# A four-block metaformer on one core: the stages behind the scan are split by image and interleaved

## The reference, cut to what matters

```python
x = x + L0_conv(ln_c(x))            # selective scan over 4 directions, projection
t = t + L0_ffn(ln_t(t))             # mixture of 8 experts, top 2, GELU
x = x + L1_conv(ln_c(x))            # neighbourhood attention, 8 heads, 7x7 window
t = t + L1_ffn(ln_t(t))             # mixture of 8 experts, top 2, GELU
x = x + L2_conv(ln_c(x))            # involution, 3x3, weights made from the pixel
t = t + L2_ffn(ln_t(t))             # switch: 8 experts, top 1, capacity 80, ReLU
x = x + L3_conv(ln_c(x))            # 1x1 projection
t = t + L3_ffn(ln_t(t))             # mixture of 16 gated experts, top 2, SiLU
```

## Time and profile before

| | us |
|---|---|
| median of 3 runs | 360.73 |
| the three runs | 361.05, 355.65, 360.73 |
| the profiled execution, whole | 356.61 |
| its span, first to last instruction | 354.8 |
| TensorE busy | 292.2 (82%) |
| VectorE busy | 233.8 (66%) |
| ScalarE busy | 146.3 (41%) |
| GpSimd busy | 119.7 (34%) |
| granted TensorE clock, mean | 0.901 |

### The profile page before, as it was taken

One profiled execution on the slowest core, in us unless ns is written; L12 is line 12 of the kernel. 1 busy time (PEld: TensorE's weight loads), 2 busy tenths in 40 slices (PEclk: granted clock), 3 DMA queues, 4 the chain that ended last, 5 costly groups with the idle time before them and its releaser, 6 DMA issues.

```text
span 354.8 us, 4098 instructions
## 1 busy us (share of the span) xinstructions
PE 292.2 (82%) x1444; PEld 129.6 (37%) x1452; DVE 233.8 (66%) x468; ACT 146.3 (41%) x285; POOL 119.7 (34%) x72
## 2 busy tenths in 40 slices
PE   6999575665577696785999889998999989987996
PEld 2433111111111232122424589873343733443322
DVE  2308899999999999957415674425155432757784
ACT  1138644433434424240454485524651066303452
POOL 3003467787887876668000043400000100020000
PEclk9699659889759969679699999998999999999998
DMA  7980000000000000013000000000000000000000
GB/s 248 358 310 0 0 3 0 0 1 2 0 0 1 2 0 0 2 32 146 0 2 0 0 3 1 2 0 2 0 1 2 0 2 0 0 0 2 2 0 15
DMA packets 5126, 10.09 MB, mean 28 GB/s; under 512 B 2689, under 2 KB 3265, under 8 KB 4850
## 3 DMA queue, kind: packets, MB, share of 16 engines
q1 hardware_dynamic: 5106, 9.84, 7.8%
HBM read 9.70 MB, written 0.13 MB: 28 GB/s over the span
## 4 chain that ended last, share of the span: by engine, by line
PE 56%; DVE 27%; issue 8%; POOL 3%; ACT 2%; DMA 1%; SPq 1%; DVEq 0%; POOLq 0%; ACTq 0%
DVE arena L1163 14%; PE ps L842 9%; PE ps L822 7%; PE ps L627 5%; DVE arena L1150 4%; PE ps L734 4%; PE ps L953 4%; PE ps L827 2%; PE ps L666 2%; PE ps L941 2%; POOL bias L430 2%; PE ps L861 2%; PE ps L636 2%; PE ps L927 2%; PE ps L808 1%
## 5 line engine op out<-in xcount | busy, mean ns | idle before, releaser
L417 POOL TENSOR_TENSOR arena<-arena 128x1024 f32<-128x1024 f32 x31 | 77.1, 2486 | 29.7 <-DVE arena L1163 25.5
L734 PE MATMUL ps<-arena 32*128 32x510 f32 x128 | 47.7, 827 | 37.1 <-DVE arena L1150 35.4
L1163 DVE TENSOR_TENSOR_SCAN arena<-ps,arena 128x1024 f32<-128x1024 f32 x32 | 73.0, 2281 | 1.6 <-ACT ps L496 1.6
L496 ACT ACTIVATE ps<-ps,aneg 128x510 f32<-128x510 f32 x64 | 39.6, 656 | 69.6 <-PE ps L734 69.6
L740 PE MATMUL ps<-arena 32*128 32x512 f32 x128 | 46.8, 815 | 1.3 <-DVE arena L1150 1.3
L391 POOL TENSOR_TENSOR rstd<-ve,mhalf 128x4 f32<-128x4 f32 (+1 forms) x8 | 8.7, 1089 | 112.2 <-DVE ve L1045 111.5
L1150 DVE TENSOR_TENSOR arena<-ps,arena 128x1024 f32<-128x1024 f32 x32 | 38.8, 1214 | 2.3 <-PE ps L740 1.9
L627 PE MATMUL ps<-idle 128*128 128x512 bf16 x145 | 35.8, 400 | 2.2 <-POOL idle L394 1.3
L734 PEld LDWEIGHTS ps<-arena 32*128 32x128 f32 x128 | 12.2, 229 | 67.6 <-DVE arena L1150 48.6
L458 ACT ACTIVATE xt<-ps 64x256 f32<-64x256 f32 (+1 forms) x8 | 3.0, 381 | 58.9 <-PE ps L636 58.9
L842 PE MATMUL ps<-arena 128*64 128x512 f32 x96 | 25.6, 611 | 0.1
(11 more groups left out here) (215 smaller groups left out, 492.6 us busy)
## 6 DMA issues: line engine op xcount, KB each, us to landing
arena<-in_w SPq DMA_DIRECT2D x5, 512.0 KB, 5.3
bias<-in_rpb SPq DMA_DIRECT2D x1, 1408.0 KB, 8.9
w<-in_w SPq DMA_DIRECT2D x2, 512.0 KB, 7.0
arena<-in_w SPq DMA_DIRECT2D x1, 1024.0 KB, 10.7
c<-in_c SPq DMA_DIRECT2D x1, 740.0 KB, 5.6
arena<-in_w_conv SPq DMA_DIRECT2D x1, 576.0 KB, 4.5
w_bc<-in_w_bc SPq DMA_DIRECT2D x1, 512.0 KB, 5.6
c<-in_c SPq DMA_DIRECT2D x1, 480.0 KB, 6.6
```

Of the source, the lines that this page charges most:

```text
L417: pool.tensor_tensor(hc[:, i % HC_SLOTS], states[i % 4], c_all, ALU.mult).then_inc(hc_done, 1)
L496: act.activation(a, a, ACT.Exp, scale=aneg[:, q:q + 1]).then_inc(exp_done, 1)
L734: pe.matmul(dst, spread[rows_, m], src, start=True, stop=True).then_inc(dspread, 1)
L1163: dve.tensor_tensor_scan(h, decay_banks(i).rearrange("p s l -> p (s l)"), h, 0.0, ALU.mult, ALU.add).then_inc(scan_done, 1)
```

## The change

Everything behind the scan is done per image: an instruction that covered 512 tokens becomes two that cover 256 (`HALF`), and what worked on four tiles works on two (`TPI`). The programs of the engines are interleaved so that one image's norm stands inside the other's expert stage. All `keep_warm` behind the scan goes but one of 17 ahead of the first expert stage (`WARM_NORM = 17`). A few other things change with it:

- A buffer for each hidden block and for each combined quarter (`hid`, `part`): the additions into `acc` on VectorE are gone in the first three expert stages, and TensorE sums four parts per image instead of two sums for both images.
- The weights are spread for two quarters at a time, and ScalarE copies both in one instruction.
- The fourth expert stage handles two experts per step (`gate_mul`, 8 steps per image with 512 columns, `combine_two`).
- GpSimd does the first norm's power ahead of adding the window to the attention bias, which is now cut in 16 pieces.
- The output leaves in two transfers.

The core of it:

```diff
-            def turn(n):
-                if n:
-                    keep_warm(WARM_NORM[n])
-                    turned(n - 1)
-                for t in range(TB):
+            def turn(n, im):
+                for t in of_image(im):
...
-                hidden(0)
...
-                    hidden(1)
-                    down(0)
-                    hidden(2)
-                    down(1)
-                    weights(0)
-                    hidden(3)
-                    weights(1)
-                    down(2)
-                    weights(2)
-                    down(3, between=True)
+                hidden(0)
+                hidden(1)
...
+                down(0)
+                hidden(2)
+                if im == 0:
+                    turn(n, 1)
+                else:
+                    turn(n + 1, 0)
+                down(1)
+                hidden(3)
+                weights(f, im, 0)
+                if stage == 5:
+                    project(0)
+                down(2)
+                weights(f, im, 1)
+                down(3)
+                turned(n + im, 1 - im)
...
+                for p in range(4):
+                    pe.wait_ge(comb, base_c + p + 1)
+                    out_sum(im, part[p], p == 0, p == 3)
...
+            def experts(f, im):
+                n = LN_OF_FFN[f]
+                router_top(f, im)
+                if im == 1:
+                    norm(n + 1, 0)
+                    normed_rows(n + 1, 0)
+                else:
+                    if f:
+                        norm(n, 1)
+                    normed_rows(n, 1)
+                router_rest(f, im)
+                if im == 0:
+                    turned(n)
+                weights_turned(f, im)
+                for p in range(4):
+                    combine(f, im, p)
...
+            for im in range(IMAGES):
+                router_top(3, im)
+                gate_mul(im, 0)
+                if im == 0:
+                    norm(6, 1)
+                else:
+                    finish(3, 0)
+                gate_mul(im, 1)
```

More of the change, by code:

```diff
@@ L655, in _ @@
             last.then_inc(fdt_ps, 1)
-            turn(0)
+            for im in range(IMAGES):
+                turn(0, im)
             got("w_in")
-            turned(0)
+            for im in range(IMAGES):
+                turned(0, im)
             pe.wait_ge(xt_padded, 1)
@@ new lines, in _, with logits_of, weights_turn @@
+            keep_warm(WARM_NORM, 5)
+            turn(1, 0)
+            turned(1, 0)
+            def logits_of(f, im):
+                n = E_OF[f]
+                for t in of_image(im):
+                    last = pe.matmul(bank(7)[:, (t % TPI) * n:(t % TPI + 1) * n], xt[:, t * P:(t + 1) * P], wr[f][:], start=True, stop=True)
+                last.then_inc(logits, 1)
+            def weights_turn(f, im):
+                e_n = E_OF[f]
+                pe.wait_ge(w_ready, IMAGES * f + im + 1)
+                for t in of_image(im):
+                    last = pe.transpose(bank(7).bitcast(BF16)[0:PARTS * e_n, (t % TPI) * P:(t % TPI + 1) * P],
+                                        wp[:, t, 0:PARTS * e_n], ident16)
+                last.then_inc(wt_ps, 1)
@@ new lines, in out_sum @@
+            def out_sum(im, v, first, end):
+                for t in range(TPI):
+                    last = pe.matmul(bank(0)[:, t * CH:(t + 1) * CH], v[:, t * P:(t + 1) * P], stack_i,
+                                     start=(first and t == 0), stop=(end and t == TPI - 1), skip_group_check=True)
+                if end:
+                    last.then_inc(out_ps, 1)
+            def experts(f, im):
+                n = LN_OF_FFN[f]
+                stage = IMAGES * f + im
+                base, base_c = 16 * stage, 4 * stage
+                got(f"wr_{f}", f"w2_{f}", f"w1_{f}")
+                logits_of(f, im)
+                if stage == 0:
@@ new lines, in values @@
+            def values(h, im):
+                u = HEADS * im + h
+                o = 32 * (h % 4)
+                pe.wait_ge(pt_sb[u % 2], u // 2 + 1)
+                for w in range(TPI):
+                    c = HALF * (h // 4) + P * w
+                    for kb in range(2):
+                        last = pe.matmul(ps[o:o + 32, 7, c:c + P], vz[:, 2 * (TPI * im + w) + kb, h],
+                                         pt[:, u % 4, (2 * w + kb) * P:(2 * w + kb + 1) * P],
+                                         start=(kb == 0), stop=(kb == 1))
+                last.then_inc(pv, 1)
@@ L1208, in router @@
                 dve.wait_ge(load["rows"], 16)
[L1209 removed]
+                dve.wait_ge(logits, stage + 1)
                 if f == 0:
[L1211 to L1214 removed]
@@ L1294, in _ @@
-            norm(1)
-            router(0)
-            for p in range(4):
-                combine(0, p)
-            finish(0)
-            norm(2)
-            dve.wait_ge(qk_ps, 2)
-            dve.tensor_scalar(kf, bank(2), col("k_b"), None, ALU.add).then_inc(k_sb, 1)
-            dve.wait_ge(q_sb, 1)
-            for h in range(0, HEADS, 2):
-                dve.tensor_scalar(qz[:, h], qf, head_mask[:, h:h + 1], None, ALU.mult).then_inc(qz_ready[0], 1)
-            dve.wait_ge(v_ps, 1)
-            v_b = row("v_b")[0:KEY_HALF].unsqueeze(1).to_broadcast([KEY_HALF, 8, CH])
```

1014 lines of the change are left out of this document (578 added, 436 removed).

## The result

| | before | changed |
|---|---|---|
| median of 4 runs, us | 359.77 | 380.99 |
| the runs | 361.05, 355.65, 360.73, 358.81 | 384.97, 381.28, 380.69, 379.28 |
| ratio, 95% interval | | 1.066 [1.059, 1.073] |
| the profiled execution, whole / span, us | 356.61 / 354.8 | 384.97 / 383.2 |
| granted clock, mean | 0.901 | 0.846 |

The kernel is slower by 6.6%, and 381 us lies above my range of 355 to 377. The profiled execution is the longest of the four; the other three have spans of 377.4 to 379.5 us at a clock of 0.858 to 0.866.

The account below looks back on a forecast made before the run. TensorE was taken to bound the kernel, with 31 us of norm gaps to hide. Stage terms summed to +3.8 on the profiled 356.6, giving 360.4; 5.1 for the clock made 365.5, and half a microsecond more 366; range 355 to 377.

Parts of the forecast that it names:

- the clock: Behind the scan, time lost to TensorE's low clock: taken as 5.1 us, as before, with bounds 0 and 15.
- the clock is low often: Rival, chance 0.25: waits of 0.4 to 1.3 us in image stages and start-ups let the clock fall; whole 375 us.
- halfway to what the scan has: Base of the clock's upper bound behind the scan: granted 0.90 on average, 20 us, less 5 beside waits, giving 15.
- GpSimd beside the first router, +1.5 us: First expert stage: bias pieces of 0.39 us and memsets delay some 8 VectorE steps, half exposed, +1.5 us.
- Up to the first logits: Projection to first logits: GpSimd's power goes first, so 5.3 to 5.5 us instead of 11.0, -5.7 us.
- Expert image stage: One image's expert stage: TensorE work 11.9 us plus waits, 14.2 us, with the third `down` 1.3 us late.
- The two covers: Inside an expert image stage: turned rows and routing weights are both ready when TensorE wants them, 0.35 us to spare.
- the cover is too short: Rival, chance 0.12: VectorE's steps and norm run 1.3 us longer, TensorE waits 1 us per image stage; whole 371 us.
- My 0.35 us: Expert image stage: spare time before TensorE wants the weights at 7.65 us, VectorE's chain of steps ending at 7.3.
- Involution: Involution stage: 6.6 and 6.3 us for the two images, 12.9 in all, -3.3 us.
- Fourth stage: Fourth expert stage: start and end don't shrink with columns and are paid per image; 44.2 against 33.0, +11.2 us.
- only VectorE's work: Rival, chance 0.11: the fourth expert stage takes VectorE's busy time of 32 us plus 3, not 44.2; whole 352 us.

Follow-up runs that it names:

- experiment 3: Changed kernel with GpSimd's bias pieces and clears moved behind the first routing weights, and products on zeros in TensorE's gaps except the last stage's; 367.4 us, ratio 1.030.
- experiment 6: For the 14 us: the kernel before with all its products on zeros behind the scan left out; 371.5 us, ratio 1.041.
- the kernel without bias: Changed kernel with GpSimd's 16 additions of the window mask to the bias left out and its three clears moved later; 380.3 us.
- all moved: Changed kernel, all work kept, GpSimd's bias pieces and first clear behind the first routing weights, other clears behind the next norm's powers; 380.7 us, ratio 1.067.
- filled alone: Changed kernel with products on zeros in TensorE's gaps, GpSimd's bias pieces and clears left beside the first router; 372.2 us, ratio 1.042.
- the better order: Last stage issues the second image's logits and first two gate pairs before the first image's output sum; added to the kernel of experiment 3, 369.8 us.
- The fully filled kernel: Kernel of experiment 3 plus the better order, and products on zeros in the last stage and ahead of the projection; 363.7 us, ratio 1.015.
- the last kernel: Kernel before with GpSimd's power first, bias and clears later, two fewer products on zeros at the first norm, 2 and 5 before late gate products; 355.6 us.

## Why the prediction was wrong

The step that failed is **the clock**: "I take the same 5.1 us; the bounds are 0 (no fall) and 15". The low clock grew from 11 to 57 us, and filling the gaps brings back 8.8 or 13.3 us of the whole. The sign I had named for it, a mean clock below 0.87, came (0.846 to 0.866). That the gaps "are many and short" was right as a description and gave no reason to price them low: behind a stretch like the one shown in experiment 3 the clock falls about every second time. I had the row for it, the fall in the second expert stage of before, and used it only against the rule of the Trainium skill, not for its price. The skill's rule ("TensorE: Matmul & The Clock Gate", section "HAM oscillation — how this bites in real kernels", no long gap between bursts) is borne out by the 5.1 us wait in the first stage; for the falls behind idles of 0.37 and 1.25 us that section would have forecast nothing, and there the measurement decides. My rival "the clock is low often" had the mechanism and its sign, with a chance of 0.25; its price was too small as well, 30 us of low clock where 57 came, so 375 instead of 381. The base for the bound, "halfway to what the scan has", had no mechanism. What was missing was the question what the filled gaps of the kernel before were worth; experiment 6 answers 14 us.

The second failed step is a term: **GpSimd beside the first router, +1.5 us**. I let 8 steps wait 0 to 0.39 us each, half exposed. The pieces took 0.52 us each, not 0.39, most steps but the reductions waited, and one cast waited out the clears (3.26 us), which my sum named without a price. The wait was 5.10 us, and with the clock behind it the stage took 13.4 us more than forecast. Undone by itself it brings back 4.8 us of the whole with the gaps filled, and nothing with them open. A rule of the Trainium skill bears on it ("SBUF — State Buffer", section "Who interferes with whom"): VectorE and GpSimd share a pair of ports, which a VectorE instruction wants when it has two inputs in SBUF (then it meets only GpSimd instructions that read SBUF) or runs in a mode that uses both ports; whichever engine issues first has the pair for its whole instruction. The trace agrees in which steps are held (those with two SBUF inputs, `tensor_scalar` and cast at 0.47 to 0.60 us, reductions at 0.17) and that the hold is about a whole piece (0.52). It goes further in one row: the cast of 3.26 us waited for three clears in a row, not for one instruction.

The other steps, against the filled kernel of experiment 3 (clock 0.92 to 1.00):

| stretch | predicted | changed | filled |
|---|---|---|---|
| to the first logits | 5.3 | 5.4 | 5.4 |
| first experts | 29.9 | 43.3 | 29.2 |
| attention | 47.2 | 48.5 | 48.3 |
| second experts | 28.4 | 29.9 | 29.2 |
| involution | 12.9 | 15.8 | 14.2 |
| third experts, projection | 30.2 | 33.1 | 31.2 |
| fourth experts | 44.2 | 44.7 | 45.3 |
| sum | 198.1 | 220.6 | 202.7 |

- Up to the first logits: right in length. Of the 5.6 us gained, 3.4 come from GpSimd's order alone; 2.2 come with the rest of the change, which halves the norm's work there and has six products on zeros fewer.
- Expert image stage 14.2 predicted, 14.5 to 14.7 measured at full clock, with the 1.26 us wait in its place. The two covers held: no idle ahead of `turn`, and the weights in time everywhere but in the first router. The rival "the cover is too short" fell: in the second expert stage of the changed kernel, image 1, VectorE's steps follow each other every 0.21 us as I had taken, the rows are there 1.2 us and the weights 1.3 us early. My 0.35 us was a slip besides: 13 steps of 0.21 behind 4.9 end at 7.6, not 7.3, which would have left nothing to spare.
- Attention: right. Its +1.1 in the filled kernel is mostly the two moved clears; with them where the change has them it takes 47.4 us at a clock of 1.00. The third stage is right too: the kernel without bias runs it at a clock of 1.00 in 30.3 us, and the +1.0 of the filled one comes with 3 us of low clock.
- Involution +1.3: sized too small. I halved its own work almost wholly (6.6 and 6.3); it takes 7.1 per image.
- Fourth stage: 44.2 was for a high clock, so the 44.7 of the changed kernel, with 11 us of low clock in it, agree by luck. Two kernels with the same program there and 3.5 us of low clock (all moved; filled alone) take 43.3 and 43.4 us; as low clock costs at most half its length, my estimate from these for a high clock is 41.6 to 43.4. The term was 1 to 2.6 us too long. With the better order and a clock of 1.00 the stage takes 42.1. The rival "only VectorE's work" (35 us) fell: what stands between the images in program order is only 2 us of it.
- The whole at a high clock: predicted 360.4. The fully filled kernel, with a better last stage, measures 363.7.

The point forecast of 366 lies near the filled kernel (367.4), not the one that was asked about. One chance was added wrongly: 0.25, 0.12 and a sixth of 0.42 make 0.44, not 0.43.

**What stays open.** With the gaps open, moving GpSimd's work or filling its wait took 6 to 14 us off the first stage and nothing off the whole; the second expert stage with the involution was the longer (48.8 to 55.8 us against 45.6) in all four such kernels. Whether that is chance in where the clock falls or has a reason, one profile each can't say; that only 16 of 27 like stretches brought a fall, and the one run of 369.2 us, speak for chance. That VectorE and GpSimd get in each other's way at SBUF is seen by durations alone; what they share no run here shows by itself. Why one open stretch brings the fall and the next like one doesn't, no run here shows. The two new edits of the last kernel were not run apart, and whether it is faster than the kernel before is open.

## What to carry to other kernels

Splitting a stage to hide a wait also splits TensorE's work into sparser stretches, and the clock is a price of its own: price every gap that loses its filling, short ones too, by a run or a row with the low clock behind it. If work is moved on GpSimd, look at what VectorE does in the same microseconds and who waits for its last step; a clear beside a chain of tiny steps can cost its whole length. And when an edit repairs its stage and the whole doesn't move, compare all the other stages with their granted clock before giving up the edit: here its 5 us in the median appeared only once the second cause was gone. If the part ahead of the change varies in length by itself, as the scan here (157.2 to 162.8 us), compare the part behind it too.

## What the runs showed of the hardware

- A CAST of 16 columns on VectorE took 3.26 us beside three GpSimd clears that follow each other, 0.48 with the clears elsewhere and the pieces left, and 0.17 with both elsewhere; most steps with two SBUF operands took 0.47 to 0.60 beside pieces of 0.52 and 0.15 to 0.18 without them, reductions 0.17 throughout.
- A stretch of 2.4 us in which TensorE was busy 0.77, with no idle longer than 1.3 us, was followed by 3.4 us at 1.2 GHz. Over five kernels a fall followed 16 of 27 such stretches, and none of 25 that were filled with products on zeros. An idle of 5.1 us was followed by about 17 us at 1.2 GHz.
- Some 60 products on zeros in gaps are worth 13 us of 381 and cost no time where it can be compared (the involution takes 14.2 us at a clock of 1.00 with and without them); those of the kernel before 14 of 358.
- The same program's low clock is not fixed: four runs of one kernel gave 380.1, 369.2, 380.6 and 381.3 us.
